# Second attention and ternary feed-forward of a two-layer block put into one instruction block, with the middle layer's maximum taken from squares

## The reference

```python
x = x + xattn0(layernorm(x), ctx)
x = x + ffn0(layernorm(x), w12, w3, gate_w)          # 8 experts, top 2
x = x + xattn1(layernorm(x), ctx, ctx, mask)         # softmax(q ctx^T / 16), masked
x = x + ffn1(layernorm(x), w1, b1, w2, b2)
# ffn1 = bitlinear(gelu(bitlinear(x, w1, b1)), w2, b2), hidden width 1024
def bitlinear(x, w, b):
    xn = x * rsqrt(mean(x*x) + 1e-6)                 # per row
    scale = 127 / clip(max(abs(xn)), 1e-5)           # per row
    xq = clip(round(xn * scale), -128, 127) / scale
    wq = clip(round(w / mean(abs(w))), -1, 1) * mean(abs(w))
    return xq @ wq.T + b
```

## Time and profile before

| | |
|---|---|
| median of 3 runs | 780.03 us (779.78 to 781.59) |
| profiled execution, own time | 777.34 us |
| its span, first to last instruction | 775.6 us |
| busy: PE, DVE, ACT, POOL | 72%, 69%, 48%, 47% of the span |
| attention stage (`attend1`) | about 488 to 623 us of the span |
| feed-forward stage (`bitffn`) | about 623 to 773 us |
| mean granted TensorE clock | 0.857 |

### The profile page before, as it was taken

One profiled execution on the slowest core, in us unless ns is written; L12 is line 12 of the kernel. 1 busy time (PEld: TensorE's weight loads), 2 busy tenths in 40 slices (PEclk: granted clock), 3 DMA queues, 4 the chain that ended last, 5 costly groups with the idle time before them and its releaser, 6 DMA issues. The chain is left out here.

```text
span 775.6 us, 18120 instructions
## 1 busy us (share of the span) xinstructions
PE 556.9 (72%) x5883; PEld 484.5 (62%) x5883; DVE 533.2 (69%) x1486; ACT 369.1 (48%) x707; POOL 366.1 (47%) x384
## 2 busy tenths in 40 slices
PE   4787736005999999999999997033656736877774
PEld 3666625005999999999999997022444513555553
DVE  6887655154777766766656564375778878999994
ACT  2598634002343334334334433224534628988883
POOL 1024264747999999995000000475644054455431
PEclk9687855557999999999999999556867969999999
DMA  6996141232222222232222221933544100010011
GB/s 213 344 362 226 59 146 52 104 116 42 61 65 66 61 69 64 63 70 63 63 66 67 64 69 42 305 100 117 164 136 135 55 0 0 29 35 34 31 46 49
DMA packets 77585, 74.76 MB, mean 96 GB/s; under 512 B 44480, under 2 KB 67904, under 8 KB 76224
## 3 DMA queue, kind: packets, MB, share of 16 engines
q1 hardware_dynamic: 71360, 56.92, 23.9%
q0 software_dynamic: 6144, 16.79, 6.7%
HBM read 40.51 MB, written 23.86 MB: 83 GB/s over the span
## 5 line engine op out<-in xcount | busy, mean ns | idle before, releaser
L911 PE MATMUL banks<-z_turned,w_of_block 128*128 128x128 f16 x3408 | 203.8, 220 | 26.5 <-DMA z_turned<-z_rows 26.5
L911 PEld LDWEIGHTS banks<-z_turned,w_of_block 128*128 128x128 f16 x3408 | 191.8, 98 | 29.6 <-DVE w_of_block L984 26.6
L992 DVE SCALAR_TENSOR_TENSOR hidden_T<-banks,blk_inv,silu_T 128x512 f32<-128x512 f32 x71 | 53.3, 751 | 99.3 <-PE banks L911 99.2
L413 POOL DMA_INDIRECT z_rows<-z_parts,places_in_regions x64 | 63.0, 984 | 104.8 <-DVE places_in_regions L719 86.7
L984 DVE COPY w_of_block<-w_parts 128x4096 f16 x71 | 98.2, 1384 | 10.4 <-issue 10.4
L957 ACT ACTIVATE hidden_T_high<-hidden_T 128x512 fp32r<-128x512 f32 x71 | 44.9, 633 | 109.2 <-DVE hidden_T L992 109.2
L924 PE MATMUL banks<-w_low,hidden_T_high 128*128 x284 | 86.0, 303 | 1.5 <-DVE hidden_T_low L998 1.5
L1107 POOL DMA_INDIRECT expert_rows_in<-expert_rows,places_of_rows x64 | 62.5, 977 | 48.2 <-DVE x_rows L1236 26.2
L950 ACT ACTIVATE silu_T<-banks,blk_inv 128x512 f32<-128x512 f32 x71 | 48.8, 688 | 72.3 <-PE banks L911 72.3
L924 PE MATMUL banks<-w_high,hidden_T_low 128*128 x284 | 79.9, 281 | 0.0
L924 PE MATMUL banks<-w_high,hidden_T_high 128*128 x284 | 79.8, 281 | 0.0
(11 more groups left out here) (235 smaller groups left out, 1297.4 us busy)
## 6 DMA issues: line engine op xcount, KB each, us to landing
expert_rows<-expert_out SPq DMA_DIRECT2D x71, 128.0 KB, 1.7
w_parts<-in_w SPq DMA_DIRECT2D x7, 1024.0 KB, 7.1
x_rows<-in_x SPq DMA_DIRECT2D x8, 512.0 KB, 5.7
c_T<-in_ctx_turned SPq DMA_DIRECT2D x16, 256.0 KB
w_low<-in_w SPq DMA_DIRECT2D x8, 512.0 KB, 8.8
c_T_in<-in_ctx_turned SPq DMA_DIRECT2D x32, 128.0 KB
c_in<-in_ctx_rows SPq DMA_DIRECT2D x32, 128.0 KB
out<-rows_out SPq DMA_DIRECT2D x32, 128.0 KB, 1.7
```

The costliest lines, as they stand in the source:

```text
L413: pool.indirect_dma_start(z_rows[:, :], bass.IndirectOffsetOnAxis(ap=put_at[:, t, k:k + 1], axis=0), zp[:, t % ZP, :], None).then_inc(scat ...
L911: mm = pe.matmul(PS[:, 1 + half + 2 * u, hc * P:(hc + 1) * P], win[:, u, wp, c, at:at + P], zT[:, j % ZB, k, :], start=(n == 0), stop=(n = ...
L992: v.scalar_tensor_tensor(out=g[:, :], in0=PS[:, 2 + 2 * u, :], scalar=blk_inv[:, j:j + 1], in1=s[:, :], op0=ALU.mult, op1=ALU.mult).then_i ...
```

## The change

`attend1` and `bitffn` become one function `layer1` with one block; the barrier between them is gone. All feed-forward loops are written out tile by tile, so that waits compare against constants. All tensors of both stages stand in SBUF at once.

- The fp16 numbers of the rounded tiles are multiplied as they are: `keep_xt` and `keep_ht` are plain copies, w1 and w2 are fp16, the scale 256 goes into `wmore`. The +6 is taken out again by products with column sums of the weights: `mid_sums1` (PE, 4 matmuls of 5 rows, ahead of attention group 7) and `mid_parts` (DVE, two 5x512 operations) for w1 through two more rows of b3; `mid_sums2` (8 matmuls of 2 rows) and `mid_parts2` for w2, used by one more 2-row matmul at the head of each `down`.
- `square` writes its squares in fp32 and `largest_h` takes the maximum of those by a tensor_scalar with an accumulator output, so it now waits for `square` and not for `gelu`. `scale_h` has 17 links as before (its two square roots side by side in width 8), but the scale for `round_h` is ready after link 14. `scale_x` has 7 links.
- `keep_ht` of every fourth tile runs on DVE. `round_h` and `turn_h` move to step t+6, `finish` to t+9. In PE's order `down(s-8)` still comes first, then `turn_h(s-6)`: the turn is now two tiles ahead of the product.
- `centre` on POOL is a tensor_scalar with a per-row mean; `add_b2` follows four steps behind through a ring of 8 and no longer waits for the latest `finish`.
- The norms of tiles 0 to 7 are computed by DVE ahead of attention's drain (`group(NR)`); those of tiles 8 to 31 after the first `scale_x`. Three memsets and one small product (`wmore`, `ialT`) stand on DVE ahead of attention's `group(0)`; POOL has four more memsets ahead of its gathers.

```diff
-                    a.activation(x1T[...], PS[:, 0, 0:P].bitcast(F16), ACT.Identity, scale=LOW_STEP, bias=magic[:, 2:3])
+                    a.activation(x1T[:, t % 2, :], PS[:, XT, 0:P].bitcast(F16), ACT.Copy)
-                    apart(dve, gelu_made, R * i + (k + 1))
-                    v.tensor_reduce(am2[:, k:k + 1], h[:, k, :], AX_X, ALU.max, apply_absolute_value=True)
+                    dve.wait_ge(sq_made, t + 1)
+                    v.tensor_scalar(sq[:, t % 2, :], sq[:, t % 2, :], 1.0, 0.0, ALU.mult, ALU.max,
+                                    accum_out=am2[:, t % R:t % R + 1])
+                def down(t):
+                    after(pe, fin_made, t - 1)
+                    wait_ht_kept(pe, t)
+                    bank = PS[:, YS[t % 2], 0:D]
+                    pe.matmul(bank, one16[0:2, :], w2mid[0:2, :], start=True, stop=False)
+                    for c in range(FC):
+                        mm = pe.matmul(bank, hT[:, t % 2, c * P:(c + 1) * P], w2q[:, c, :], start=False, stop=(c == FC - 1))
+                for s in range(T + LATE):            # PE, LATE = 10
+                    if s + 1 < T: turn_x(s + 1)
+                    if s < T: up(s)
+                    if s % Q == 1 and s + 3 < T: turn_b(s // Q + 1)
+                    if 0 <= s - 8 < T: down(s - 8)
+                    if 0 <= s - 6 < T: turn_h(s - 6)
+                dve.wait_ge(mean_made, 2)            # DVE, ahead of the attention's groups
+                v.tensor_scalar(wmore[:, :], wmean[:, :], LOW_STEP / 127.0, None, ALU.mult)
+                v.memset(ialT[:, :, :].bitcast(F32), 0.0)
+                dve.wait_ge(bt_set, 2)
+                v.memset(ialT[0:5, :, :].bitcast(F32), 1.0)
+                group(0)
+                with dve.Fori(1, NR - 1) as i:
+                    group(i)
+                group(NR - 1)
+                mid_parts()
+                mid_parts2()
+                early = ffn_norms(0, R, 0)
+                advance(early, NORM_N)
+                group(NR)
+                dve.wait_ge(bt_set, 3)
+                for t in range(R):
+                    largest_x(t)
+                advance(scale_x(0), L1)
+                late = ffn_norms(R, T, NORM_N)
+                advance(late, 4)
+                keep_b(0)
+                advance(late, NORM_N)
+                for s in range(T + LATE):
+                    if s % Q == 0 and s + Q < T:
+                        chain_x = scale_x(s // Q + 1)
+                        advance(chain_x, 2)
+                    if 0 <= s - 6 < T: round_h(s - 6)
+                    advance(chain_x, 1); advance(chain_h, 3)
+                    if 0 <= s - 1 < T: largest_h(s - 1)
+                    advance(chain_x, 1); advance(chain_h, 3)
+                    if 0 <= s - 7 < T and by_dve(s - 7): keep_ht(s - 7)
+                    if s % Q == 0 and 0 < s <= T:
+                        advance(chain_h, L2)
+                        chain_h = scale_h(s // Q - 1)
+                        advance(chain_h, 3)
+                    if 0 <= s - 9 < T: finish(s - 9)
+                    advance(chain_x, L1); advance(chain_h, 3)
+                    if s % Q == 2 and s + 2 < T: keep_b(s // Q + 1)
+                    if s + R < T: largest_x(s + R)
```

More of the change, by code:

```diff
@@ new lines, in up @@
+                def up(t):
+                    if t % Q == 0:
+                        pe.wait_ge(bt_kept, t // Q + 1)
+                    after(pe, gelu_made, t)
+                    pe.wait_ge(xt_kept, t + 1)
+                    for c in range(DC):
+                        for half in range(2):
+                            pe.matmul(PS[:, 1 + half, :], x1T[:, t % 2, c * P:(c + 1) * P],
+                                      w1q[:, c, half * 512:(half + 1) * 512], start=(c == 0), stop=False)
+                    for half in range(2):
+                        mm = pe.matmul(PS[:, 1 + half, :], ialT[:, t // Q % 2, (t % Q) * P:(t % Q + 1) * P],
+                                       b3[:, half * 512:(half + 1) * 512], start=False, stop=True)
+                    mm.then_inc(h_made, 1)
@@ new lines, in _ @@
+                pe.wait_ge(w2_mid, 1)
+                turn_x(0)
+                turn_b(0)
+                pe.wait_ge(qt_kept, T)
+                pe.wait_ge(ne_made, T)
+                pe.wait_ge(pt_kept, T)
+                pe.wait_ge(x3_made, T)
+                for s in range(T + LATE):
+                    if s + 1 < T:
+                        turn_x(s + 1)
+                    if s < T:
+                        up(s)
+                    if s % Q == 1 and s + 3 < T:
+                        turn_b(s // Q + 1)
+                    if 0 <= s - 8 < T:
+                        down(s - 8)
+                    if 0 <= s - 6 < T:
+                        turn_h(s - 6)
@@ L1690, in _, with keep_ht @@
-                advance(norms(), NORM_N)
-                v.memset(ialT[:, :, :].bitcast(F32), 0.0).then_inc(bt_zero, 1)
-                for k in range(Q):
-                    largest_x(0, k)
-                advance(scale_x(0, 0), L1)
-                for k in range(Q, R):
-                    largest_x(0, k)
-                dve.wait_ge(bt_zero, 1)
-                keep_b(0, 0)
-                schedule(dve, group)
+                def keep_ht(t):
+                    after(dve, y_made, t - 1)
+                    dve.wait_ge(ht_made, t + 1)
+                    v.tensor_copy(hT[:, t % 2, :], PS[:, 3 + t % 2, :].bitcast(F16)).then_inc(ht_kept_dve, 1)
@@ new lines, in finish, with mid_parts @@
+                def finish(t):
+                    after(dve, o_out[t % Q], 16 * (t // Q))
+                    dve.wait_ge(links2, L2 * (t // Q + 1))
+                    dve.wait_ge(xb_made, t + 1)
+                    dve.wait_ge(y_made, t + 1)
+                    v.scalar_tensor_tensor(out=fin[:, t % Q, :], in0=PS[:, YS[t % 2], 0:D], scalar=be[:, t % R:t % R + 1],
+                                           in1=xb[:, t % R, :], op0=ALU.mult, op1=ALU.add).then_inc(fin_made, 1)
+                def mid_parts():
+                    dve.wait_ge(w_mid, 1)
+                    for half in range(2):
+                        cols = slice(half * 512, (half + 1) * 512)
+                        v.tensor_tensor(b3[0:5, cols], PS[0:5, 6 + half, :], b3[0:5, cols].bitcast(F32), ALU.add)\
+                            .then_inc(b3_mid, 1)
@@ new lines, in _ @@
+                advance(late, 4)
+                keep_b(0)
+                advance(late, NORM_N)
+                chain_h, chain_x = iter(()), iter(())
+                for s in range(T + LATE):
+                    if s % Q == 0 and s + Q < T:
+                        chain_x = scale_x(s // Q + 1)
+                        advance(chain_x, 2)
+                    if 0 <= s - 6 < T:
+                        round_h(s - 6)
+                    advance(chain_x, 1)
+                    advance(chain_h, 3)
+                    if 0 <= s - 1 < T:
+                        largest_h(s - 1)
+                    advance(chain_x, 1)
+                    advance(chain_h, 3)
+                    if 0 <= s - 7 < T and by_dve(s - 7):
+                        keep_ht(s - 7)
+                    if s % Q == 0 and 0 < s <= T:
+                        advance(chain_h, L2)
+                        chain_h = scale_h(s // Q - 1)
+                        advance(chain_h, 3)
+                    if 0 <= s - 9 < T:
+                        finish(s - 9)
+                    advance(chain_x, L1)
+                    advance(chain_h, 3)
+                    if s % Q == 2 and s + 2 < T:
+                        keep_b(s // Q + 1)
+                    if s + R < T:
+                        largest_x(s + R)
```

497 lines of the change are left out of this document (222 added, 275 removed).

## The result

The changed kernel takes 784.43 us (median of 20 runs, 778.04 to 790.09) against 779.76 for the kernel before on the same chip: ratio 1.0054, interval 1.0031 to 1.0077. It is slower by about 4 us where 4.5 us faster was forecast. Its profiled execution has a span of 779.8 us (775.6 before), which divides as follows; "masked" is the start of the operation by which VectorE masks the scores of a tile, "first gelu", "step 12" and "step 32" are starts of the gelu and of VectorE's `round_h` in that step.

A forecast was written before the change was run, and what follows sets the result against it. VectorE was taken to set the steady pace, with ScalarE bounding the first tiles and a serial drain. Start +1.7, seam 0, ramp -1.2, middle +2.5, drain -7.5 summed to -4.5: 775.5 us from 780.03, own range 771 to 780.

The forecast's parts named there:

- (e): Steady state: VectorE's remaining waits for the port POOL holds, kept unchanged, -0.6 to +0.8 us for each four tiles.
- rival 1: Steps 12 to 32: VectorE pays more than the drain gives back, +2.2 for four tiles, +11 over five, 784 us; chance 0.20.
- `largest_h` +0.2 for four tiles: Steady state: the accumulating maximum costs 1.18 us against the reduce's 1.13, so +0.2 us for four tiles.
- `keep_ht` 0.87: Steady state: one copy on VectorE for four tiles, +0.87 us, the middle between 0.6 and 1.14.
- (c) and (d): Steady state: shorter `scale_x` and the 17 links of `scale_h` on VectorE, together -0.35 us for four tiles.
- the size +2.5: Step 12 to step 32: five times four tiles at +0.5 us each, with all ends -11 to +9.
- Ramp, -1.2 forecast: First steps up to `round_h` of step 12: start at 674.3 against 675.52 us, -1.2 (0 to -2.5).
- The late norms, costed at nothing: Between `keep_b(0)` and step 0: some 2.5 us, covered while PE and ACT work; without cover they cost all.
- Seam, 0 forecast: Attention's end to the first `up`: gain and loss cancel, 0 us, between -2 and +2.
- Start, +1.7 forecast: Start of attention: one small product and two memsets on DVE cost +1.7 us, between 0 and +2.1.
- Drain, -7.5 forecast: Step 32 to the end: 15.2 us instead of 22.7 at TensorE's 1.6 us a tile, 7.5 saved (3 to 9).
- Rivals 2 and 3: Accumulating maximum runs like `round_h`, 766 us, chance 0.12; drain saves only 3 of 7.5, 780 us, chance 0.18.

The follow-up runs named there:

- before_no_b2: The kernel before without `add_b2` (output bias b2 left out, `finish` takes the row X1 itself): middle 72.2 us, ratio 0.9954 to the kernel before.
- no_b2: The changed kernel without `add_b2` (output bias b2 left out, `finish` takes the row X1 itself): middle 8.5 us shorter, ratio 0.9895 to the kernel before.
- b2_paced: The changed kernel with `add_b2` on GpSimd waiting for the `finish` of four tiles before, not of eight: steps 12 to 32 take 79.57 us.
- fin_late: The changed kernel with `finish` moved behind the third group of links of its step on VectorE: steps 12 to 32 take 79.30 us.
- fin_late_paced: The changed kernel with both fin_late's and b2_paced's edits: middle 76.83 us, 133.75 us from the first gelu to the end.
- mid_early: The changed kernel with `mid_sums1/2` and `mid_parts/2` one attention group earlier: seam 3.1 us shorter, first gather to last `masked` but one 118.0 us against 112.9.
- after_again: The changed kernel run once more with no edit, as yardstick: 139.64 us from the first gelu to the end, 137.40 in its first trace.
- before_swap: The kernel before, with `turn_h` ahead of the previous tile's `down` in TensorE's order in the last group only: drain 24.0 us against 22.7.

## Why the prediction was wrong

The step that failed is (e) of the steady state: "POOL has as many operations as before, so I keep them". The number of operations was right and said nothing; what each `add_b2` meets on VectorE was put at nothing. before_no_b2 and no_b2 price it: 2.9 us before, 8.5 after, +5.6 over the five times four tiles, +1.1 for each four where -0.6 to +0.8 was allowed. Part of the cause is the order: in the changed kernel three dependent links stand behind `finish`, and GpSimd runs ahead in bursts (`add_b2` waits for a finish eight tiles back). Each edit alone gave nothing (b2_paced +0.3, fin_late 0.0), both together (fin_late_paced) 2.5 us of the middle and 1.9 of the ramp. So 2.5 of the 5.6 are shown to be order, 1.7 are idle time that came back in the kernel before, and for the rest no run names the cause.

By stages the forecast of -4.5 misses the +4.3 of the traces by 8.8 us: the ramp has 4.7 of it, the middle 1.9, the drain 1.9, the seam 1.8, the start -1.5. The largest is therefore the second step that failed, the ramp, whose sum followed VectorE alone (below).

The time of rival 1 (784) came true by luck. Its mechanism, GpSimd on the links in bursts, is what the runs show, and its point of decision was just crossed: four tiles cost 16.9 to 17.0 us. But it wanted +2.2 for four tiles and +11 for the middle, where +1.0 in the steady part and +4.4 in all were measured; it had 0.4 of waiting where 1.1 came, and copy and accumulating form at 1.2 and 1.3 us where they cost 0.60 and 1.13. The ramp, the seam and the drain made up the difference.

Two sums of the prediction don't come out of their own terms. For four tiles +0.2, +0.87 and -0.35 make +0.7, not +0.5: +3.6 over five instead of +2.5. In the drain three turns of 1.6, the last copy, product and `finish` make 7.3 us behind `round_h(28)`, or 8.9 with a whole turn of tile 28, where 8.7 stands.

The rest of the middle, by its terms:
- `largest_h` +0.2 for four tiles: 0.0 (1.13 net in both). The row of attention overstated it.
- `keep_ht` 0.87: 0.60, the lower of the two bounds.
- The links of (c) and (d), -0.35: without `add_b2` -2.0 over five, -0.4 each. Right.
- Not forecast: `round_h` is cheaper by 2.3 us in all, since it is held less. Counted alone it would look like a gain.
- So without `add_b2` the middle is 1.4 us shorter than before, not 2.5 longer: VectorE's instructions come to 68.5 and 68.6 us, copy included, and the changed kernel idles 1.5 us less. That the size +2.5 was near +4.4 is luck, two errors of opposite sign.

The Trainium skill (SBUF — State Buffer, Who interferes with whom) has the two engines share one port pair as an exclusive lock, which the other waits out for the whole instruction, with reduces and the accumulator form exempt. The rows agree: the links that meet `add_b2` end with it to 0.03 us, and in no trace is `largest_x` over 0.42 us or `largest_h` over 1.22. They differ on the whole instruction in one place: GpSimd's centring as a `tensor_scalar` lasts 0.92 us and let a link go after 0.50 (last section).

Ramp, -1.2 forecast, +3.5 measured: I followed VectorE's own sum and not TensorE, which in its fixed order waits for a `round_h` asked for a step earlier than VectorE can give it. The hole is 3.13 us against 1.44. The late norms, costed at nothing, also push the next `scale_x` (1.4 us) past the first gelu: the last of them ends at 640.3. But VectorE then idles 0.52, 1.15 and 0.56 us in front of the next three `largest_h`, so the delay is at least in part taken in. The lower clock behind the hole cost nothing, by mid_early. fin_late_paced brings the ramp to 39.28: of the 3.9 us by which after_again is longer 1.9 go with its two edits, so they were contention, and 2.0 are left. no_b2 has 39.85, of which 1.2 are its slow first tile, so some 2.0 above before_no_b2 again. How these 2.0 divide between hole, late norms and the copy no run shows.

Seam, 0 forecast, +1.8 measured, inside the -2 to +2 given. The sum took the norms of eight tiles at 3.3 us; they took 5.0 with GpSimd's centring beside them, which is the work they were to hide. Start, +1.7 forecast: its 2.4 us are there and attention takes nearly all of it in.

Drain, -7.5 forecast, -5.6 measured (3 to 9 given). The pace of 1.6 us is right. `round_h(28)` started 7.2 us after step 32's start (at 767.73), so it ended after 7.9 and not 6.5, with one link stretched to 0.71 us by `add_b2`; what follows it took 9.2 and not 8.7. before_swap shows what I had wrong in the reasoning: TensorE's order alone gives nothing; the later `finish` on VectorE is the other half.

Rivals 2 and 3 are out: 1.14 us for the accumulating maximum, and the drain did shorten.

## What to carry to other kernels

When two engines lock each other out, don't count operations, look at what each one falls on: an operation released by X hits what stands behind X, so put there what wasn't hit in these runs (reduces, the accumulator form) or what loses least (one wide operation), not a row of tiny dependent ones. Time it: of the two edits of this kind, each alone gave nothing here. This drain was set by a ring of orders on two engines; look for such a ring, and open it in the last steps, where the steady state is left alone. Before an in-order engine is given a step earlier, check that its producer has it a whole step earlier too.

## What the runs showed of the hardware

- A small VectorE link of 0.17 us lasts up to 0.73 us beside a GpSimd `tensor_tensor` with two SBUF inputs (`add_b2`, 0.72 us). `round_x`, a GpSimd `tensor_scalar` of 0.48 us with one input, holds links too, up to 0.43 us.
- GpSimd's centring costs VectorE less as a `tensor_scalar`, although that is longer (0.94 against 0.61 us; middle 0.8 to 0.9 us shorter in both kernels). As a `tensor_tensor` it holds a link to its own end; as a `tensor_scalar` it mostly lets go about half-way: in the seam of the changed kernel the link that starts at 622.48, 0.09 us behind the first centring, ends at 622.89, when that centring has some 0.4 us to go.
- The same GpSimd subtraction is slower as `tensor_scalar` with a per-partition number (0.94) than as `tensor_tensor` with that number broadcast (0.61).
- VectorE's copy of 128x1024 fp16 numbers out of PSUM: 0.685 us, 0.60 to the next start, as much as 512 fp32 columns.
- ScalarE's plain copy of 1024 columns takes 1.02 us, the affine one 1.11.
